# A bidirectional Mamba layer: the output projection moved into the scan's loops, step sizes computed first, one transposing product per iteration, channel halves interleaved over the partitions

## The reference, cut to what matters

```python
E, N, R, K = 256, 64, 8, 4                       # D = 128, batch 8, T = 256
xp, z = split(x @ W_in.T)                        # 256 + 256 channels
xc = silu(conv_K(xp) + conv_b)
dt_lo, Bm, Cm = split(xc @ W_xp.T)               # 8, 64, 64
dt = softplus(dt_lo @ W_dt.T + dt_b);  A = -exp(A_log)
h  = exp(dt * A) * h + (dt * xc) * Bm            # for each of 256 x 64 states, along t
y  = sum_n(h * Cm) + xc * Dp
y  = (y * silu(z)) @ W_out.T
out = layernorm(mamba1(xn) + flip(mamba2(flip(xn)))) * w2 + b2 + xn
```

## Time and profile before

| | us |
|---|---|
| median of 3 runs | 4481.45 (4477.12 to 4491.47) |
| the profiled execution | 4477.53 |
| its span, first to last instruction | 4475.7 |
| scan, first direction | 619.6 |
| scan, second direction | 615.0 |

### The profile page before, as it was taken

One profiled execution on the slowest core, in us unless ns is written; L12 is line 12 of the kernel. 1 busy time (PEld: TensorE's weight loads), 2 busy tenths in 40 slices (PEclk: granted clock), 3 DMA queues, 4 the chain that ended last, 5 costly groups with the idle time before them and its releaser, 6 DMA issues. The chain is left out here.

```text
span 4475.7 us, 81436 instructions
## 1 busy us (share of the span) xinstructions
PE 3578.2 (80%) x25981; PEld 2270.9 (51%) x25981; DVE 3269.6 (73%) x5840; ACT 2354.3 (53%) x5437; POOL 2500.5 (56%) x2256
## 2 busy tenths in 40 slices
PE   5888888888856876875888999548888884898984
PEld 3666666666645655654744677313343441343443
DVE  4777777777737756855622788669999957999985
ACT  2555555555524433433333666456767655667661
POOL 2555555555535414414411334429999926999982
PEclk8999999999967887887989999666666675656666
DMA  1000000000000000000000000049998927998870
GB/s 55 9 9 9 9 9 9 9 9 9 8 18 0 0 21 1 0 9 3 0 27 19 1 1 1 24 139 229 228 228 223 226 60 197 230 224 228 225 183 34
DMA packets 196430, 326.80 MB, mean 73 GB/s; under 512 B 95904, under 2 KB 125872, under 8 KB 194224
## 3 DMA queue, kind: packets, MB, share of 16 engines
q1 hardware_dynamic: 196144, 323.29, 28.5%
HBM read 304.30 MB, written 18.87 MB: 72 GB/s over the span
## 5 line engine op out<-in xcount | busy, mean ns | idle before, releaser
L3517 ACT ACTIVATE banks<-banks,alog 128x255 f32<-128x255 f32 x2048 | 788.2, 448 | 361.8 <-DVE h L3598 201.3
L3447 PE MATMUL banks<-dt_rows,selectors 96*128 96x510 bf16 x1024 | 521.5, 542 | 239.5 <-ACT banks L3517 150.9
L3598 DVE TENSOR_TENSOR_SCAN h<-banks,dBx 128x1024 f32<-128x1024 f32 x256 | 573.5, 2269 | 69.0 <-ACT banks L3517 64.3
L3576 POOL TENSOR_TENSOR dBx<-residual,b_by_state 128x1024 f32<-128x1024 f32 x256 | 597.8, 2356 | 46.0 <-DVE h L3598 21.5
L3576 POOL TENSOR_TENSOR norm_featmajor<-norm,b_by_state 128x1024 f32<-128x1024 f32 x256 | 598.8, 2359 | 10.2 <-DVE h L3598 8.7
L3598 DVE TENSOR_TENSOR_SCAN h<-banks,norm_featmajor 128x1024 f32<-128x1024 f32 x256 | 575.2, 2270 | 28.4 <-ACT banks L3517 25.1
L3462 PE MATMUL banks<-h,c_spread 128*32 128x128 f32 x8192 | 481.1, 376 | 10.7 <-DVE h L3598 8.3
L3462 PEld LDWEIGHTS banks<-h,c_spread 128*32 128x32 f32 x8192 | 273.8, 144 | 260.7 <-issue 206.3
L3447 PEld LDWEIGHTS banks<-dt_rows,selectors 96*128 96x128 bf16 x1024 | 121.8, 128 | 529.1 <-ACT banks L3517 432.9
L973 POOL TENSOR_TENSOR weighted<-probs,f 128x1024 f32<-128x1024 f32 x64 | 120.8, 1904 | 215.4 <-DVE f L1024 214.2
L2611 POOL TENSOR_TENSOR out_factors<-out_norms,exponents 128x4 f32<-128x4 f32 x64 | 64.5, 1008 | 288.3 <-DVE out_norms L2776 288.3
(11 more groups left out here) (451 smaller groups left out, 8816.4 us busy)
## 6 DMA issues: line engine op xcount, KB each, us to landing
residual<-mamba_dtx_rows SPq DMA_DIRECT2D x512, 256.0 KB, 4.4
norm<-mamba_dtx_rows SPq DMA_DIRECT2D x512, 256.0 KB, 4.3
mamba_dt_rows<-dt_parts SPq DMA_DIRECT2D x8, 768.0 KB, 3.9
dt_rows<-mamba_dt_rows SPq DMA_DIRECT2D x32, 192.0 KB, 5.1
delta_blocks<-A_turned SPq DMA_DIRECT2D x256, 8.0 KB, 1.5
inv_turned<-delta_blocks SPq DMA_DIRECT2D x256, 8.0 KB, 1.8
mamba_dtx_rows<-dtx SPq DMA_DIRECT2D x16, 256.0 KB, 4.7
c_spread<-in_l3a_zero SPq DMA_DIRECT2D x2, 1160.0 KB, 6.8
```

What stands on the lines that cost most here:

```text
L3447: nc.tensor.matmul(out, mem["sel"][:, 2 * row:2 * row + 2, :].rearrange("r g n -> r (g n)"), rows[:, kh, 2 * x:2 * x + 2, 1:], start=True, ...
L3517: e = fn(per_step(decay[l % 2])[:, 2 * x + j, 1:], k.bank[x][:, j * T + 1:(j + 1) * T], ACT.Exp, scale=mem["A"][:, at:at + 1])
L3576: nc.gpsimd.tensor_tensor(per_step(dBx[l % 4]), per_step(kept[l % 4]), across(mem["B"][:, tokens(tb)], 4), ALU.mult).then_inc(q["dbx"], 1)
L3598: v.tensor_tensor_scan(flat(h[:, u % 2, 4 * i:4 * i + 4, :]), decay[l % 2], dBx[l % 4], 0.0, ALU.mult, ALU.add).then_inc(q["scanned"], 1)
```

## The change

`mamba_output` is gone. Its work is done inside the scan, an element at a time and one element late: `gate` writes into a new tile `gated` (for m = 2 reversed), after l = 26 in place of 18; at l = 28 `project` on TensorE multiplies by `W_out` into the bank that the gate has read, for m = 2 with the first direction's result added by a product with the identity; at l = 30 ScalarE's `output` copies it to `k.Y`. X and H are loaded back by SP at the end of the second scan, and H is scaled by GpSimd in the first direction's `mamba_inputs`, before it is stored. `turn` runs once in each iteration from l = 9 to 24; `y_tokens` is doubled, and so TensorE's and ScalarE's loops run over pairs of elements. The wait for the zeros in `c_spread` stands at l = 5 of the first element, and its first builds at l = 5, 6, 10 and 11, as in the others. In `mamba_inputs` the rows of `dt_low` are computed and copied ahead of B and C, and ScalarE copies C as well. The two channel halves are interleaved over the partitions (state n of half g on partition 2n + g), so a load of dt * xc writes every second partition, and `build` works on all 128 with a 0/1 mask as its scale.

```diff
-        mem["sp"].dma_start(mem["kept"][n % 4][g * 64:(g + 1) * 64, :],
+        mem["sp"].dma_start(mem["kept"][n % 4][g::SE, :],
...
-                    sp.dma_start(mem["kept_h"], k.H[:]).then_inc(q["kept"], 16)
                     sp.wait_ge(q["reversed"], 1)
                     sp.dma_start(mem["reversed"], rev[:]).then_inc(q["kept"], 16)
+                    sp.wait_ge(q["h_scaled"], 1)
+                    sp.dma_start(mem["kept_h"], k.H[:]).then_inc(q["kept"], 16)
...
                 project_x(3)
+                low(0)
                 project_z(2)
-                rows(0)
+                low(1)
                 project_z(3)
-                rows(1)
+                low(2)
                 steps(0)
-                rows(2)
                 steps(1)
-                rows(3)
+                low(3)
+                b_and_c(0)
                 steps(2)
+                b_and_c(1)
                 steps(3)
+                b_and_c(2)
+                b_and_c(3)
...
                 if m == 1:
                     nc.gpsimd.tensor_copy(rev[:], k.HT[:, :, PAD + T - 1:PAD - 1:-1]).then_inc(q["reversed"], 1)
+                    nc.gpsimd.tensor_tensor(k.H[:], k.H[:], across(mem["affine"][:, 0, :], NT), ALU.mult)
+                    pool.drain()
+                    nc.gpsimd.tensor_tensor(k.H[:], k.H[:], across(mem["affine"][:, 1, :], NT), ALU.add).then_inc(q["h_scaled"], 1)
...
                 def next_dtx(n):
-                    sp.wait_ge(q["dbx"], n + 1)
+                    sp.wait_ge(q["dbx"], n - 3)
...
+                if m == 2:
+                    sp.wait_ge(q["dbx"], B * NS)
+                    sp.dma_start(k.X[:], mem["kept_x"]).then_inc(q["back"], 16)
+                    sp.dma_start(k.H[:], mem["kept_h"]).then_inc(q["back"], 16)
+                    sp.wait_ge(q["back"], 32)
...
+                def project(tb):
+                    pe.wait_ge(q["gated"], tb + 1)
+                    for half in range(2):
+                        out = k.bank[YBANK][:, half * D:(half + 1) * D]
+                        if m == 2:
+                            nc.tensor.matmul(out, k.ident[:], k.Y[:, bass.ds(2 * tb + half, 1), :].rearrange("p n d -> p (n d)"),
+                                             start=half == 0, stop=False)
+                        for e in range(SE):
+                            i = nc.tensor.matmul(out, gated[:, e, half * P:(half + 1) * P], mem["wout"][:, e, :],
+                                                 start=m == 1 and half == 0 and e == 0, stop=half == 1 and e == SE - 1)
+                    i.then_inc(q["out"], 1)
...
-                        if NI < l <= 2 * NI and not first:
-                            x = l - NI - 1
-                            turn(tb - 1, x // 2, x % 2 * 2)
-                            turn(tb - 1, x // 2, x % 2 * 2 + 1)
+                        if NI < l <= 3 * NI and not first:
+                            turn(tb - 1, 1 - par, (l - NI - 1) // 4, (l - NI - 1) % 4)
+                        if l == NS - 4 and not first:
+                            project(tb - 1)
...
+                def output(tb):
+                    act.wait_ge(q["out"], tb + 1)
+                    act.sem_inc(q["through_act"], 1)
+                    fn(k.Y[:, bass.ds(2 * tb, 2), :], k.bank[YBANK][:, 0:2 * D].rearrange("p (n d) -> p n d", d=D), ACT.Copy).then_inc(q["y_read"], 1)
...
-                        if l in builds and not first:
+                        if l in builds:
+                            if first and l == min(builds):
+                                act.wait_ge(q["spread_zeroed"], 16)
                             build(tb, *builds[l])
+                        if l == NS - 2 and not first:
+                            output(tb - 1)
 
                 act.wait_ge(q["zeroed"], 1)
-                act.wait_ge(q["spread_zeroed"], 16)
-                for half in range(2):
-                    for g in range(SE):
-                        build(0, half, g)
...
-                        z = sz[:, g, tokens(tb)]
-                        i = v.tensor_tensor(z, by_token(g), z, ALU.mult)
-                    i.then_inc(q["y_read"], 1)
+                        dst = gated[:, g, :] if m == 1 else gated[:, g, ::-1]
+                        i = v.tensor_tensor(dst, by_token(g), sz[:, g, tokens(tb)], ALU.mult)
+                    i.then_inc(q["gated"], 1)
...
-                        if l == 2 * NI + 2 and not first:
+                        if l == 3 * NI + 2 and not first:
                             gate(tb - 1)
```

More of the change, by code:

```diff
@@ L3037, in mamba_memories @@
     m["sp"] = k.nc.sync
-    m["sel"] = p.sb("selectors", [SROWS, 32, 64], BF16)
-    m["self"] = p.sb("selectors_f32", [SROWS, 32])
+    m["sel"] = p.sb("selectors", [SROWS, 16, 64, SE], BF16)
+    m["self"] = p.sb("selectors_f32", [SROWS, 16, SE])
+    m["half"] = p.sb("halves", [P, SE])
     R = D // 16
@@ L3366, in _ @@
                 softplus(1)
-                copy_c(3)
                 positive_part(2)
@@ L3398, in mamba_scan @@
         ROWS, DTX = (m - 1) * 16 * B, (m - 1) * 32 * B * NS // 4
-        ysb = p.sb("y_tokens", [P, NG, P, 4])
-        names = ("zeroed", "cast", "decayed", "dbx", "scanned", "chunked", "built", "moved", "y_ready", "y_read", "spread_zeroed",
-                 "through_pool")
+        ysb = p.sb("y_tokens", [P, 2, NG, P, 4])
+        gated = p.sb("gated", [P, SE, T])
+        names = ("zeroed", "cast", "decayed", "dbx", "scanned", "chunked", "built", "moved", "y_ready", "gated", "out", "y_read", "back", "spread_zeroed",
+                 "through_pool", "through_act")
         q = {n: p.sem(n) for n in names}
```

205 lines of the change are left out of this document (86 added, 119 removed).

## The result

The kernel before, timed again beside the changed one, took 4479.28 us (median of 4 runs, 4474.21 to 4491.47), the changed kernel 4423.4 us (4 runs, 4406.84 to 4434.47): a ratio of 0.9869 with a 95% interval of 0.9841 to 0.9898. The prediction was 4419.7, within 4400 to 4452. The profiled execution of the changed kernel took 4426.8 us, with a span of 4425.0; the step sums of the prediction gave 4415.8 for it. Of all the executions behind this document, three far-off slow ones (9237 and 5544 us of the kernel before, 15853 us of the variant `staged`) are left out of the ratios.

What follows compares the result with a forecast made beforehand. TensorE was taken to bound eight iterations of an element, the ScalarE/VectorE pair 24, GpSimd close behind. Gains 17.5 + 16.3 + 11.5 + 11.1 + 4.7 + 0.6 = 61.7 us gave 4415.8 profiled, 4419.7 median; range 4400 to 4452.

Steps and rivals of the forecast that it cites:

- The loop over pairs: TensorE's and ScalarE's scan loops: twice the code in a pass of the loop, given no cost.
- One turn per iteration: Scan elements: sixteen single-turn iterations of 2.46 us instead of eight double ones; element 74.4 us instead of 76.08.
- Start of a scan: First element of a scan: GpSimd never stops, as exponentials precede the zeros' wait; 4.5 us gained, some 3.5 in the second.
- The stall while the weights load: First scan, while the second direction's weights load: DMA waits kept at 4.5 us.
- Projection in the loop: Project at l = 28 in each element: costs 0 in the first direction, 0.2 us in the second; bound 2 us.
- Output part: Between last gate and next part: separate output work goes, 11.5 us gained in the first direction, 11.1 in the second.
- Step sizes first: Input phases: rows of dt_low computed first and C copied by ScalarE; 4.7 us gained in the second direction, bounds 0.6 and 6.
- Scaling of H beside the convolution: First inputs: two GpSimd products hold VectorE, in the worse order twice, eating the 4.1 us; 0.6 gained, bounds -3 and +4.5.
- A: Scan elements: spreading the turns gives nothing, element stays near 76.1 us; 36 us gained in all, 4445; chance 0.18.
- B: Scan loop: project holds it, a late gate costs 2 us in 14 elements, 28 us; 4448; chance 0.06.
- C: Scan elements: GpSimd becomes the only bound, 73.9 us an element, convolution held once; 4409; chance 0.12.
- D: Scan loads: interleaving lengthens them; 13% longer eats the whole gain, 20% gives 4557, slower; chance 0.04.

Runs made afterwards that it cites:

- staged: Changed kernel with one body per element again on TensorE and ScalarE, moves of units 0 and 1 staged and copied by ScalarE; 4411.9 us, 0.9855 of the kernel before.
- unrolled: Changed kernel with the pair loops of TensorE and ScalarE written out as straight code; 4398.2 us, 0.9822 of the kernel before.
- staged_again: The same kernel as staged, run once more; 4414.1 us, 0.9868 of the kernel before.
- staged_blocks: Against staged: the two channel halves in blocks of 64 partitions again instead of interleaved; 4423.4 us, 0.9874 of the kernel before.
- staged_two: Against staged: the turns again two in each of eight iterations; 4446.0 us, 0.9935 of the kernel before.
- staged_h_tail: Against staged: scaling of H moved from the first inputs to GpSimd in the tail of the second scan; 4407.8 us, 0.9837 of the kernel before.
- half_chunks: Against the changed kernel: each chunk of C times h does half its matmuls, pair loops kept, work left out; 4399.4 us, one run.
- act_one: Against the changed kernel: only ScalarE's loop brought back to one body, TensorE keeps the pair loop; 4424.1 us, 0.9890 of the kernel before.

## Why the prediction held, and the step of it that failed

The forecast case came, but that it lies 3.7 us from the number is partly luck: the layer gained 47.2 us where the sum had 61.7. Step by step:

- **The loop over pairs: failed.** "The loops now run over pairs of elements, with twice the code in a turn of the loop; the trace shows no idle time at a loop's end that this could add to, and I give it nothing." The trace showed what a jump back to held code costs, and I read it as the cost of any jump. Measured: a branch of 4.9 to 5.8 us in place of 0.215. Against unrolled, the same code without back edges, the last six elements lost 8.2 and 4.6 us in the first profile of the changed kernel and 10.9 and 4.9 in the second: 13 to 16 us in both scans together. Two scans of one kernel (the first of staged and of staged_again) differ by 6.7 us there, so the size is rough; it is most of the 15 us missing.
- **One turn per iteration: the mechanism right, the size off.** An iteration with a turn takes 2.47 us (I had 2.46). But the element is 75.06 us in unrolled, where I had 74.4 and 74.6: 3.6 and 2.9 us a scan too short. Of the 5.3 us above 32 x 2.18, the turns have 4.0 and the gate 0.65, as summed. The rest, some 0.6, stands at the element's start. In unrolled, by stretch, some three iterations each:

```profile
3855.00:3861.20 6.20, 3.70 (x50) 1.32 (x38) 6.20 (x3) 5.21 (x14) 6.20 (x4) 1.00 0.71 221
3861.20:3868.00 6.80, 6.58 (x56) 3.20 (x56) 6.76 (x5) 4.71 (x13) 6.80 (x4) 0.51 0.81 257
```

  The clock falls to the lower level there, a chunk takes 1.08 us instead of 0.65, and the two products of `by_d` make TensorE late. In the kernel before the clock stood high at that place.
- **Start of a scan: right in kind, a little large** (2 to 4 us for 4.5 and 3.5).
- **The stall while the weights load: too dear by 1 to 4 us.** I kept the 4.5 us of before; element 1 ended earlier than summed by 4.1 us in one profile of the changed kernel and 1.3 in the other; in staged_blocks, with slower loads, it ended 4 to 5 us later than in staged. Interleaving was the part of the change that I gave "nothing".
- **Projection in the loop: right, as far as one profile tells.** 0.2 to 0.6 us an element in staged_two against 0 and 0.2; the longest wait for `gated` in the first scan of the changed kernel was 0.6 us.
- **Output part: right.** 11.1 and 10.9 for 11.5 and 11.1; the copy took 0.38 us instead of 0.6.
- **Step sizes first: right, slightly small.** 5.5 for 4.7 in the second direction. ScalarE's first exponential of the softplus stands 31.8 us into the phase where it stood at 34.9: 3.1 us, where I had 4.1. The rest comes later in the phase, and no run parts the order of the rows from the copy of C.
- **Scaling of H beside the convolution: right.** Held twice, worse order, cost 4.3 us of the 5.6 that the phase would have gained. The first held step ends with GpSimd's instruction (2916.36 and 2916.27), the second 0.5 us after it. The Trainium skill, "SBUF — State Buffer", section "Who interferes with whom", says that the one who loses stands for the whole of the other's instruction, and these rows agree.
- **Rivals.** A and B are priced above and didn't come. C did not come in the changed kernel, where GpSimd waited for VectorE's scans 9.6 and 6.3 us in the two scans. But it is real: in the first scan of staged_again and in the second of staged_h_tail GpSimd never waited for VectorE, and the last six elements took 443.9 and 444.3 us, 74.0 each, which is its pace. D is contradicted.

So of 61.7 us, 12.8 went at the back edges, 6.5 were not there in the elements as unrolled ran them, and some 4 came in addition (the weights' stall and the inputs). The median lay nearer than the profile (4423.4 against 4419.7, 4426.8 against 4415.8) because a shift of 3.9 us from profile to median was carried over, and the real one had the other sign; that is scatter, and together the two brought the number nearer by 7.3 us.

## What to carry to other kernels

When a change doubles the body of a loop, count the instructions in a pass per engine before pricing it at nothing: TensorE jumped back over 1303 to 1633 records in 0.2 us and over 2606 to 2657 in some 5, at some jumps with a second stall behind it, and ScalarE stood up to 2.0 us after a jump over 489. If a buffer's parity forces a doubled body, a small copy on an engine with idle time, or straight code, can be cheaper than the pair. And price work by its neighbour as well as by itself: two hidden GpSimd products cost 4.3 us beside VectorE's convolution and nothing in a tail.

## What was not expected of the hardware

**A long jump back costs 5 us on TensorE, straight new code nothing that shows.** This is told above. ScalarE's pair loop had a stall of its own, 1.7 to 2.0 us at each jump back, seen only in half_chunks, where TensorE's is gone and GpSimd's pace hid it; what it would cost in the full kernel with TensorE's stall gone is not shown.

**The same code in the same place runs at two rhythms.** The busy time of staged_again by element of the first scan, elements 1 to 5 (PEclk is the third number from the end):

```profile
3074.10:3151.60 77.50, 72.72 (x621) 33.77 (x620) 73.18 (x36) 53.95 (x139) 75.75 (x33) 0.57 0.75 239
3151.60:3225.10 73.50, 66.15 (x621) 31.98 (x620) 71.61 (x36) 53.92 (x140) 73.50 (x33) 0.69 0.74 232
3225.10:3297.80 72.70, 65.98 (x621) 31.64 (x620) 71.61 (x35) 54.03 (x140) 72.70 (x33) 0.69 0.73 232
3297.80:3373.50 75.70, 70.92 (x621) 33.27 (x620) 72.90 (x36) 53.90 (x140) 75.70 (x34) 0.59 0.73 232
3373.50:3447.40 73.90, 68.66 (x621) 33.00 (x620) 71.82 (x35) 53.97 (x140) 73.90 (x33) 0.65 0.76 233
```

The work is the same in each row, but for the stall of the first while the next weights load. At a mean granted clock of 0.57 to 0.59 the element took 75.7 us and more, at 0.69 it took 72.7 to 73.5. An element can be shorter than GpSimd's 73.9 if filled buffers are left from the one before; over the last six the mean is 74.0, and GpSimd has no idle time in the last four of these rows: the quick rhythm is rival C's. In unrolled and in staged's first run the elements settled instead at 75.0 to 75.2 us with 0.61 to 0.66, and stayed there for both scans. Which rhythm a scan falls into moved it by up to 8 us (605.1 in staged and 597.5 in staged_again), as much as the back edges cost. What decides it stays open. A disturbed element (a back edge, a late load) was in several scans followed by quicker ones at a higher clock, as in act_one and staged_blocks, so a stall is partly given back: in the changed kernel VectorE lost 18.7 us at the back edges, and its last six elements are 12.8 us longer than unrolled's. How much is given back in general, these runs do not tell.
